# Causal attention with latent keys rewritten: pairs of heads side by side, blocks of 256 queries, queries rotated in turned layout, no loop

## What is computed

```python
B, S, E, H = (2, 256, 256, 16)          # S is 1024 in the inputs drawn
NOPE, ROPE, VD = (128, 64, 128); LORA = 64
q = (x @ wq).reshape(b, s, H, QH).transpose(0, 2, 1, 3)
q_nope, q_pe = (q[..., :NOPE], q[..., NOPE:])
kva = x @ wkv_a
ckv, k_pe = (kva[..., :LORA], kva[..., LORA:])
...
q_pe = _rope(q_pe, cos, sin)             # x1*cos - x2*sin, x2*cos + x1*sin
...
scores = jnp.einsum('bhqd,bhkd->bhqk', qs, ks_) * scale
scores = jnp.where(causal, scores, jnp.finfo(scores.dtype).min)
attn = jax.nn.softmax(scores, axis=-1)
out = jnp.einsum('bhqk,bhkd->bhqd', attn, v)
return out.transpose(0, 2, 1, 3).reshape(b, s, H * VD) @ wo
```

## Time and profile before

| | |
|---|---|
| median of three runs | 1471.77 us (1463.14 to 1471.78) |
| profiled execution, its own time | 1471.49 us |
| its span | 1469.1 us |
| mean granted clock of PE | 0.949 |
| collect | 448.0 to 490.8 us |
| attention, batch 0 | 490.80 to 898.65 us |
| of it: opening | 25.12 us |
| of it: seven pairs of heads, each followed by the next one's preparation | 344.66 us |
| of it: last pair | 38.07 us |
| output and next keys | 898.65 to 942.00 us |
| attention, batch 1 | 942.00 to 1349.10 us |

### The profile page before, as it was taken

One profiled execution on the slowest core, in us unless ns is written; L12 is line 12 of the kernel. 1 busy time (PEld: TensorE's weight loads), 2 busy tenths in 40 slices (PEclk: granted clock), 3 DMA queues, 4 the chain that ended last, 5 costly groups with the idle time before them and its releaser, 6 DMA issues. The chain is left out here.

```text
span 1469.1 us, 23884 instructions
## 1 busy us (share of the span) xinstructions
PE 1278.5 (87%) x7096; PEld 966.7 (66%) x7097; DVE 973.3 (66%) x2055; ACT 655.6 (45%) x1183; POOL 826.6 (56%) x654
## 2 busy tenths in 40 slices
PE   6974699999983599999999997789999999998797
PEld 5863455555552477777677776767777777777686
DVE  4568522222224859888778886868888888976657
ACT  3221233333320356655555654246565655665242
POOL 2026778888874355555555556445555555555554
PEclk9976799999995899999999999999999999999999
DMA  9358245555554000000000000000000000002001
GB/s 326 115 159 214 90 65 82 80 81 79 81 72 133 15 1 9 8 7 0 8 7 0 1 1 12 8 8 8 8 0 7 7 7 0 0 1 60 5 8 51
DMA packets 66218, 67.13 MB, mean 46 GB/s; under 512 B 15040, under 2 KB 59648, under 8 KB 66016
## 3 DMA queue, kind: packets, MB, share of 16 engines
q1 hardware_dynamic: 48048, 42.38, 9.8%
q0 software_dynamic: 15168, 20.72, 9.1%
q10 hardware_dynamic: 2928, 3.15, 0.7%
HBM read 45.12 MB, written 21.10 MB: 45 GB/s over the span
## 5 line engine op out<-in xcount | busy, mean ns | idle before, releaser
L1525 POOL TENSOR_TENSOR att_prob_lo<-att_prob,att_prob_hi 128x896 fp32r<-128x896 f32 (+1 forms) x192 | 383.6, 1998 | 194.9 <-ACT att_prob_hi L1472 194.9
L1386 PE MATMUL all_bank<-att_q_hl,sequence_k_hl 128*128 128x512 f32 (+2 forms) x1152 | 282.5, 354 | 5.8 <-DVE att_minus L1593 5.7
L1578 DVE TENSOR_REDUCE att_peak<-all_bank 128x1 f32<-128x512 f32 (+3 forms) x384 | 207.6, 549 | 72.5 <-PE all_bank L1373 54.3
L1406 PE MATMUL all_bank<-att_prob_hi,sequence_v_hl 128*128 128x512 f32 (+2 forms) x768 | 231.1, 384 | 7.5 <-ACT late_oT L1481 7.4
L1465 ACT ACTIVATE att_prob<-all_bank 128x896 f32<-128x896 f32 (+1 forms) x192 | 162.8, 848 | 148.4 <-PE all_bank L1392 147.8
L1386 PEld LDWEIGHTS all_bank<-att_q_hl,sequence_k_hl 128*128 128x128 f32 x1152 | 193.1, 191 | 24.9 <-DVE att_minus L1593 7.1
L1370 PE MATMUL all_bank<-sequence_k_hl,att_q_hl 128*128 128x512 f32 (+3 forms) x384 | 168.3, 441 | 11.1 <-DVE att_peak L1578 10.9
L1472 ACT CAST att_prob_hi<-att_prob 128x896 fp32r<-128x896 f32 (+1 forms) x192 | 168.6, 878 | 2.5
L1519 POOL TENSOR_TENSOR att_rows<-att_by_cos,att_by_sin 128x128 f32<-128x128 f32 x128 | 58.6, 458 | 182.9 <-DVE att_by_sin L1564 182.9
L903 PE MATMUL all_bank<-early_w_gu,moe_xgT 128*128 x316 | 148.8, 553 | 3.6 <-issue 2.4
L868 POOL DMA_INDIRECT sums<-moe_y,early_slot_far x79 | 125.4, 1587 | 36.4 <-issue 18.8
(11 more groups left out here) (246 smaller groups left out, 2288.0 us busy)
## 6 DMA issues: line engine op xcount, KB each, us to landing
sequence_w_raw<-wqk_rows SPq DMA_DIRECT2D x16, 256.0 KB, 2.7
early_w_gu<-in_gate SPq DMA_DIRECT2D x16, 224.0 KB, 5.9
early_w_gu<-in_up SPq DMA_DIRECT2D x16, 224.0 KB, 6.1
early_w_down<-in_down SPq DMA_DIRECT2D x1, 3584.0 KB, 19.8
sums<-early_zero SPq DMA_DIRECT2D x18, 128.0 KB, 3.5
all_xT<-in_xT SPq DMA_DIRECT2D x4, 512.0 KB, 8.7
all_x_tok<-in_x SPq DMA_DIRECT2D x1, 2048.0 KB, 16.8
x_rows<-all_x_tok SPq DMA_DIRECT2D x4, 512.0 KB, 3.0
```

The lines of the kernel that those rows point to most:

```text
L1386: nc.tensor.matmul(ps, k_hl[:, ks, j * P:(j + 1) * P], q_hl[r // 2 % 2][:, qs, r % 2, q0:q0 + w], start=n == 0, stop=False)
L1406: mm = nc.tensor.matmul(pv_ps[:, q0 - qc * WIDE:WIDE], v_hl[:, vs, j, :], part[:, x % 3, a:z], start=j == 0 and n == 0, stop=last and n == 2)
L1525: nc.gpsimd.tensor_tensor(prob_lo[:, x % 3, a:z], prob[:, x % 2, a:z], prob_hi[:, x % 3, a:z].bitcast(F32), ALU.subtract).then_inc(lo_sb, 1)
L1578: nc.vector.tensor_reduce(peak[:, r % 2, n, i:i + 1], max_ps[y % 2][:, 0:w], AX_X, ALU.max).then_inc(peak_sb, 1)
```

## The change

`phase_attention` is written anew (L1230 to L1632 of the changed kernel), without a loop: all steps are written out.

Two heads of a pair now lie side by side in every product. Queries go in four blocks of 256, so 512 columns are 256 queries of either head. A pair has ten steps (block i, key tiles 2jj and 2jj+1, jj up to i), with 768 columns of scores where i = jj and 1024 else. The number of matmuls of a pair falls from 288 to 212.

Queries are projected already turned: weights stationary, tokens moving, in four chunks per pair (head, half of the tokens) of six matmuls of 512 columns (L1340). The transposes go. The rotation uses tables laid out in the same way (`turned_table`, 128 x 2 x 1024 float32, loaded by one more transfer of SP at the end of `phase_collect`; cosine is 1 for the unrotated rows): ACT copies the rotated rows with their halves exchanged (`swap`, L1441 and L1442, 32 partitions each), DVE multiplies the projected rows from PSUM with the cosine (`by_cos`, L1565), POOL multiplies the exchanged ones with the sine (L1510) and adds (L1513), ACT rounds (`q_high`, L1450), POOL subtracts (`q_low`, L1520; before, DVE did it from PSUM).

PSUM: the scores keep banks 0 to 3, values alternate between 4 and 5, and query chunks and maxima pieces ("items beside") share 6 and 7 in the order in which they come. An item waits until what stood two before it was read (`bank_free`): by `by_cos` for a chunk, by DVE's reduction for a piece.

```diff
+    NEXT_PIECES = [0, 0, 1, 2, 3, 3, 3, 3, 3, 3]
+    OWN_PIECES = [2, 1] + [0] * (NG - 2)
+    DIVIDE_AT = {2: 0, 4: 1, 7: 2, 1: 3}
...
+                def bank_free(item):
+                    a = place[item]
+                    if a < 2:
+                        return
+                    kind, n, v = order[a - 2]
+                    if kind == "query":
+                        pe.wait_ge(raw_sb, n * QC + v + 1)
                     else:
-                        by_pair(pe, rows_sb, u, r, QT, t)
-                        by_pair(pe, q_lo_sb, u, r, QT, max(t - 1, 0))
-                    n = 0
+                        pe.wait_ge(peak_sb, n * NP + v + 1)
...
-                def turn(u, r, t):
...
+                    if ahead:
+                        scores(u + AHEAD, 0)
+                    for item in beside_it[0:1]:
+                        beside(item)
                     if ahead:
-                        scores(*ahead, 0)
-                    for y in peak_pieces[:1]:
-                        max_piece(u, r + 1, y)
-                    if made:
-                        queries(u, *made)
+                        scores(u + AHEAD, 1)
+                    for item in beside_it[1:2]:
+                        beside(item)
+                    values(u, 0)
+                    for item in beside_it[2:3]:
+                        beside(item)
+                    values(u, 1)
+                    for item in beside_it[3:]:
+                        beside(item)
...
             @block.scalar
+                    if made:
+                        swap(n + 1, x)
+                    if u + AHEAD < STEPS:
+                        probs(u + AHEAD)
+                        highs(u + AHEAD)
+                    if made:
+                        q_high(n + 1, x)
+                    if x in last_of:
+                        sums(n, last_of.index(x))
...
             @block.gpsimd
+                    pool.wait_ge(swap_sb, c + 1)
+                    nc.gpsimd.tensor_tensor(own, own, sin[:, cols], ALU.mult).then_inc(sin_sb, 1)
+                    pool.wait_ge(raw_sb, c + 1)
+                    pool.wait_ge(sin_sb, c + 1)
+                    nc.gpsimd.tensor_tensor(raw[:, c % 2], raw[:, c % 2], own, ALU.add).then_inc(rot_sb, 1)
...
+                    if n + 1 < PAIRS:
+                        if 1 <= x <= QC:
+                            q_low(n + 1, x - 1)
+                        if x < QC:
+                            rotate(n + 1, x)
+                    if u + AHEAD < STEPS:
+                        low(u + AHEAD)
...
             @block.vector
+                def by_cos(n, k):
...
+                    dve.wait_ge(swap_sb, c + 1)
+                    if c >= 2:
+                        dve.wait_ge(q_lo_sb, c - 1)
+                    nc.vector.tensor_tensor(raw[:, c % 2], bank_of(("query", n, k)), cos[:, cols], ALU.mult
+                                            ).then_inc(raw_sb, 1)
```

More of the change, by code:

```diff
@@ L1303, in is_round @@
[L1303 to L1320 removed]
+        pv_ps = [bank[:, n, :] for n in (4, 5)]
@@ L1322, in phase_attention, with bank_of, chunk @@
+        aside_ps = [bank[:, n, :] for n in (6, 7)]
+        def bank_of(item):
+            return aside_ps[place[item] % 2]
+        def chunk(k):
+            return k % 2, k // 2
         with nc.Block() as block:
@@ new lines, in query @@
+                def query(item):
+                    _, n, k = item
+                    h, c = chunk(k)
+                    bank_free(item)
+                    if n:
+                        pe.wait_ge(w_sb, n)
+                    i = 0
+                    for xs, ws in ((0, 0), (0, 1), (1, 0)):
+                        for kc in range(KC):
+                            mm = nc.tensor.matmul(bank_of(item), w_hl[:, ws, kc, h * P:(h + 1) * P],
+                                                  x_hl[:, xs, kc, c * WIDE:(c + 1) * WIDE],
+                                                  start=i == 0, stop=i == 3 * KC - 1)
+                            i += 1
+                    mm.then_inc(q_mm, 1)
@@ L1443, in _, with beside @@
-                turn(0, 1, 0)
-                scores(0, 0, 1, 1)
-                rounds(pe, step)
+                def beside(item):
+                    (query if item[0] == "query" else piece)(item)
+                for k in range(QC):
+                    query(("query", 0, k))
+                for y in range(8):
+                    piece(("piece", 0, y))
+                scores(0, 0)
+                scores(0, 1)
+                for y in range(8, EARLY):
+                    piece(("piece", 0, y))
@@ new lines, in beside @@
+                def beside(item):
+                    kind, n, v = item
+                    if kind == "query":
+                        by_cos(n, v)
+                    else:
+                        peaks(n, v)
+                        if v + 1 in block_needs:
+                            spread(n, block_needs.index(v + 1))
+                dve.wait_ge(turned_loaded, 16)
+                for item in opening:
+                    beside(item)
+                weights_high(1)
+                weights_low(1)
```

605 lines of the change are left out of this document (267 added, 338 removed).

## The result

The changed kernel takes 1509.43 us (median of four runs, 1500.97 to 1511.57) against 1471.7 before: a ratio of 1.026, 95% interval 1.0206 to 1.0315. It is slower by 2.6%; the forecast was 1511.

The account below looks back on a forecast made before the run. PE bounds the kernel; POOL's load in steps 0 to 3 makes it wait. 1471.5 + 2 × (opening 1.1 + seven pairs of 52.5 + last pair 34 − 382.73) = 1511 us, range 1440 to 1540.

Parts of the forecast that it names:

- PE's work: Matmuls of a pair: 47.31 us busy falls to 43.4, between 44.3 by columns alone and 42.8 with a fixed 25 ns each.
- The walk: Steps 0 to 3 of a pair: PE waits for banks that late by_cos frees; with 0.8 later, 43.4 becomes 51.0 us.
- The clock: After a pair's longest new wait PE's granted clock falls to half: 1.5 us added per pair, bounds 0 and 3.
- Rival 1: DVE's waits for POOL in steps 0 to 3 fall off the chain: pair 47.8 us, total 1445, faster; chance 0.17.
- The opening: Before an attention's first pair: step 0 starts at about 517 instead of 515.92, +1.1 us, bounds −2 and +4.
- The last pair: Pair with no next one to prepare: 29.2 us of PE, 3.95 idle and 0.9 for last sums, 34 us.

Follow-up runs that it names:

- tenth kernel: Changed kernel without DVE's division products and POOL's product with the sine, block 1's sums on ACT behind step 3's swap: 1410.29 us, 0.958 of before.
- eleventh kernel: Changed kernel, all work kept: DVE multiplies with the sine from PSUM, POOL does division products, reciprocals later, weights earlier, chunks before pieces: 1416.88 us, 0.965 of before.
- twelfth kernel: The eleventh kernel with the opening's first four chunks in PSUM banks 0 to 3 and four pieces reduced ahead of the last by_cos: 1414.91 us, 0.964 of before.
- fourth kernel: Changed kernel with q_low moved from POOL back to DVE, both inputs in SBUF, in the opening too: 1538.39 us, 1.051 of before.
- eighth: Changed kernel, all work kept: DVE multiplies with the sine from PSUM, POOL does the division's products, chunks before pieces: 1452.55 us, 0.990 of before.

## Why the prediction was right

The sum was met with 1509.43 for 1511, in part by luck: two misses cancel.

**PE's work.** Forecast 43.4 us a pair; 42.65 to 42.81 in the tenth and eleventh kernel, with the clock at 1.00, so the matmuls' fixed part was nearer the truth (42.8) than columns alone. In the changed kernel PE is busy 45.18 in the first of the pairs shown and 43.81 in the second, whose clock is 1.00: 1.4 us are the clock's. About 1 us more is there at full clock too; its cause is open.

**The walk.** Forecast losses 0.8, 1.2, 1.0, 3.8 in steps 0 to 3 and 0.8 later; measured 0.69, 0.94, 1.09, 2.74 and 1.22 (waits for reductions in steps 5 to 7; the walk had a division in steps 4 and 5). Place, order and releaser were right, the last one a microsecond too long; the times of `by_cos` 2 and 3 came out at 17.9 to 18.5 and 23.7 to 24.4 us after step 0 where the walk had 18.8 to 19.5 and 25.7 to 26.4.

**The clock.** Forecast 1.5 us; the window behind the 2.74 has 2.81 us busy of 2.90 at 0.50, so 1.4 there, and 1.4 by the busy times of the two pairs above. Smaller than the waits, but most long waits carry it: in the tenth kernel it was half of the gain. With it the pair adds up: 43.8 + 5.5 + 1.2 + 1.4 = 51.9.

**Rival 1** had the right mechanism at the wrong price. It counted on the waits of DVE falling away for 4.7 us; leaving out eight of the 15 operations, the division products, gives 1, since POOL and ACT hold the same `by_cos`. The prediction's text has both chains in its walk, but priced the removal of one as if the other weren't there.

**The opening** is the term that failed: +1.1 forecast (bounds −2 and +4), +6.85 and +4.5 measured. `q_high` of the last chunk ended as worked out (508.5 forecast, 509.30 measured). But the first eight pieces and block 0's scores, which the sum took for done by then, were not: in the shared banks they are queued behind `by_cos` 2 and 3. That is a part of the miss only: other banks gave back 2.3 and 2.7 us in the twelfth kernel. The rows are PE's first two pieces and DVE's `by_cos` 3 that releases the second:

```profile
503.02 0.45 PE L1352 MATMUL all_bank<-sequence_k_hl,att_q_hl 128*128 128x128 f32 x1 [2.82 <-DVE all_xT L1565]
...
506.86 0.47 PE L1352 MATMUL all_bank<-sequence_k_hl,att_q_hl 128*128 128x128 f32 x1 [3.26 <-DVE all_xT L1565]
```
```profile
506.12 0.69 DVE L1565 TENSOR_TENSOR all_xT<-all_bank,sequence_cst_turned 128x512 f32<-128x512 f32 x1 [3.15 <-POOL att_q_hl L1520]
```

They follow after 506.86, at a granted clock of 0.50 from 508 to 516. What the clock and the chain of rotation add to the miss stays open.

**The last pair** was forecast at 34 and took 30.99: PE 28.32 busy (29.2 forecast) and 2.67 idle, not 4.85. Why it idles less than before (3.95) stays open; its last low is not shorter (768 columns instead of 512). Opening and last pair together miss by 5.75 − 3.0 = 2.7 us in the first attention, pairs by −2.4 (7 × 0.35).

**Which engine.** An operation of 128x512 takes 1.29 on POOL and 0.69 on DVE. The Trainium skill (GPSIMD Engine Reference, section 4.1 Engine selection) speaks for VectorE for elementwise work like the rotation's; the trace agrees on the price. The fourth kernel shows where that ends here: `q_low` from SBUF on DVE waits for POOL (up to 2.81, at 602.03), and the kernel became slower. From PSUM, as in the eighth, the products with the sine don't wait (0.69 to 0.70 each in the whole run).

## What to carry to other kernels

Where an operation waits for two chains of similar length, taking work off one of them gives nearly nothing; walk both to the same instruction, and cut both, or judge neither by its own trial. Place the operations that wait for another engine (here DVE's with two SBUF inputs, while POOL works) behind the one that TensorE waits for, not ahead of it. And count a long wait of PE with the slower clock that mostly follows.
